# A feature network's large product recast as seven block products (one level of Strassen's algorithm)

## The reference

```python
w = jnp.einsum('bpf,mf->bpm', features, W_ft) + b_ft      # features (1024, 2, 5128), W_ft (512, 5128)
accumulator = stm * w                                     # stm (1024, 2, 1)
l1_x = jnp.clip(accumulator, 0.0, 1.0).reshape(features.shape[0], -1)
l2_x = jnp.clip(l1_x @ W1.T + b1, 0.0, 1.0)               # W1 (32, 1024)
return l2_x @ W2.T + b2                                   # W2 (1, 32)
```

## Time and profile before

| | |
|---|---|
| Time, median of 3 runs | 455.06 us (453.8 to 456.36) |
| Profiled execution, first to last instruction (span) | 452.5 us |
| Median of the runs less that span | 2.56 us |
| PE busy | 447.9 us (99%) |
| VectorE (DVE) busy | 178.2 us (39%) |
| ScalarE (ACT) busy | 132.3 us (29%) |
| Moved by DMA | 64.55 MB, mean 143 GB/s |
| Granted TensorE clock, mean | 0.999 |

### The profile page before, as it was taken

One profiled execution on the slowest core, in us unless ns is written; L12 is line 12 of the kernel. 1 busy time (PEld: TensorE's weight loads), 2 busy tenths in 40 slices (PEclk: granted clock), 3 DMA queues, 4 the chain that ended last, 5 costly groups with the idle time before them and its releaser, 6 DMA issues.

```text
span 452.5 us, 5442 instructions
## 1 busy us (share of the span) xinstructions
PE 447.9 (99%) x1996; PEld 365.8 (81%) x1996; DVE 178.2 (39%) x202; ACT 132.3 (29%) x167; POOL 14.6 (3%) x33
## 2 busy tenths in 40 slices
PE   8999999999999999999999999999999999999997
PEld 5888888888888888888888888888888888888883
DVE  3543333333333333563853333333333333333154
ACT  5443322222222233532133222222222333322101
POOL 4800000000000000000000000000000000000000
PEclk9999999999999999999999999999999999999999
DMA  7996454444454544444264444444444444440000
GB/s 288 240 370 210 139 139 139 145 143 152 142 152 144 150 152 139 139 141 139 70 211 140 141 140 143 150 146 148 144 151 152 148 139 139 139 139 0 0 1 0
DMA packets 24180, 64.55 MB, mean 143 GB/s; under 512 B 3172, under 2 KB 3436, under 8 KB 24044
## 3 DMA queue, kind: packets, MB, share of 16 engines
q1 hardware_dynamic: 23340, 62.93, 44.4%
q0 software_dynamic: 832, 1.51, 1.2%
HBM read 64.42 MB, written 0.00 MB: 142 GB/s over the span
## 4 chain that ended last, share of the span: by engine, by line
PE 98%; DMA 1%; ACT 0%; SPq 0%; DVE 0%; issue 0%
PE sums L309 96%; PE sums L343 1%; PE sums L395 1%; DMA x_raw<-x_t 1%; ACT part L234 0%; ACT x_hi L214 0%; PE sums L403 0%; SPq L149 0%; SPq L147 0%; PE sums L409 0%; DVE res L303 0%; DVE hid L299 0%
## 5 line engine op out<-in xcount | busy, mean ns | idle before, releaser
L309 PE MATMUL sums<-x_hi,w_hi 128*128 128x512 f32 x640 | 200.1, 389 | 0.5 <-ACT x_hi L214 0.5
L309 PE MATMUL sums<-x_hi,w_lo 128*128 128x512 f32 x640 | 199.7, 389 | 0.0
L309 PE MATMUL sums<-x_lo,w_hi 128*128 128x512 f32 x640 | 199.7, 389 | 0.0
L279 DVE TENSOR_TENSOR w_lo<-w_raw,w_hi 128x512 fp32r<-128x512 f32 x79 | 54.7, 693 | 222.3 <-ACT w_hi L222 222.3
L309 PEld LDWEIGHTS sums<-x_hi,w_hi 128*128 128x128 f32 x640 | 120.1, 188 | 26.7 <-ACT x_hi L214 0.8
L309 PEld LDWEIGHTS sums<-x_lo,w_hi 128*128 128x128 f32 x640 | 120.0, 188 | 25.1 <-issue 0.4
L309 PEld LDWEIGHTS sums<-x_hi,w_lo 128*128 128x128 f32 x640 | 120.1, 188 | 24.9
L222 ACT ACTIVATE w_hi<-w_raw 128x512 fp32r<-128x512 f32 x79 | 49.9, 631 | 280.5 <-PE sums L309 275.3
L282 DVE TENSOR_TENSOR x_lo<-x_raw,x_hi 128x1024 fp32r<-128x1024 f32 x79 | 96.8, 1226 | 26.7 <-ACT x_hi L224 26.3
L224 ACT ACTIVATE x_hi<-x_raw 128x1024 fp32r<-128x1024 f32 x79 | 82.6, 1046 | 8.6 <-DMA x_raw<-x_t 8.5
L250 DVE SCALAR_TENSOR_TENSOR act<-sums,b_ft_col,stm_all 128x512 f32<-128x512 f32 x16 | 12.0, 750 | 13.9 <-PE sums L309 13.7
(11 more groups left out here) (35 smaller groups left out, 23.2 us busy)
## 6 DMA issues: line engine op xcount, KB each, us to landing
x_raw<-x_t SPq DMA_DIRECT2D x79, 512.0 KB, 3.5
w_raw<-w_t SPq DMA_DIRECT2D x79, 256.0 KB, 2.7
stm_all<-stm POOLq DMA_DIRECT2D x1, 1024.0 KB, 12.0
x_raw<-x_t SPq DMA_DIRECT2D x2, 256.0 KB, 3.0
xr_raw<-x_t POOLq DMA_DIRECT2D x4, 64.0 KB, 7.5
w_raw<-w_t SPq DMA_DIRECT2D x1, 192.0 KB, 3.3
w_sb<-w_t POOLq DMA_DIRECT2D x1, 128.0 KB, 12.2
w_raw<-w_t SPq DMA_DIRECT2D x1, 64.0 KB, 1.9
```

Of the source, the lines that this page charges most:

```text
L279: nc.vector.tensor_tensor(w_lo[:, j, :], w_raw[:, j, :], w_hi[:, j, :].bitcast(F32), ALU.subtract).then_inc(w_lo_ready, 1)
L309: return nc.tensor.matmul(sums[:, m, c, :], w[:, j, m * P:(m + 1) * P], x[:, j, c * BANK:(c + 1) * BANK], **flags)
```

## The change

Of the 5128 features, 5120 are paired as 20 pairs of tiles of 128, and the 8 left over go in 16 matmuls as before (`K_PAIRS` = 20, `x_rest`). The 512 units are cut in two blocks of 256, the rows in two blocks of 1024. With A the weights (2x2 blocks, units by features) and B the features (2x2 blocks, features by rows), the product is made of seven block products instead of eight, in the form with shared block sums (Winograd's):

- Pass 0 (steps 0 to 19): A11 B11 in banks 0 to 3, and S1 T1 in banks 4 to 7, with S1 = A21 + A22, T1 = B12 - B11. VectorE also keeps S2 = S1 - A11 for all 20 pairs, and T1 stays in SBUF.
- Pass 1 (20 to 39): S2 T2 is added to banks 0 to 3, S3 T3 goes to banks 4 to 7, with S3 = A11 - A21, T3 = B22 - B12 and T2 = B22 - T1; T2 and T3 are made by one instruction of 2 x 1024 columns with B22 broadcast, and T2 takes T1's place.
- Pass 2 (40 to 59): (A12 - S2) B22 in banks 0 to 3 and A22 (B21 - T2) in banks 4 to 7.
- Pass 3 (60 to 69): the seventh product, A12 B21; a step takes two feature tiles of it.

A step is again 24 matmuls of 128x512, and there are 70 instead of 80. Each of the first 60 steps now has 512 columns of `w` and 2048 columns of `x` to round and to subtract (hi and lo), where a step of before had 512 and 1024. The raw ring has 4 slots (`RAW`), the hi ring 3 (`HI`), and the lo parts are written over the raw slots; so a load waits for TensorE to finish the step 4 earlier (`step_done`), no longer for VectorE. Loads of passes 0 to 2 are 1.44, 1.31 and 1.31 MB a step, of pass 3 1.31 MB. In DRAM the blocks lie beside each other for each feature row (`x_p`: rows of 16 KB, of which a DMA takes 4 or 8 KB; `w_p`: rows of 4 KB).

ScalarE drains the banks after each of passes 0 to 2, 8 copies from PSUM each; VectorE adds the blocks together in pass 2 and early in pass 3 (`combine`, `finish`). The first 3 steps are split in six half steps (`open_products`, order `OPEN_HALVES`, both sums of a step behind its plain half). Three quarters of the first small layer (12 of the 16 matmuls) come before the last step, the rest behind it. `stm` (1 MB, broadcast) is loaded by SP at step 50; GpSimd's 19 other DMAs wait until two steps are done.

The core of the diff:

```diff
+K_PAIRS = 20
+COLS = 1024
+MH = 256
+PASSES = 3
+STEPS = PASSES * K_PAIRS + K_PAIRS // 2
+OPEN = 3
+RAW = 4
+HI = 3
+OPEN_HALVES = ((0, 0), (1, 0), (0, 1), (2, 0), (1, 1), (2, 1))
+
+HALVES = (((0, 0, 0), (1, 1, 4)), ((1, 1, 0), (0, 0, 4)), ((1, 0, 0), (0, 1, 4)), ((0, 0, 0), (1, 1, 0)))
+
+
...
+            for g in range(OPEN, STEPS):
+                f, k = pass_of(g)
+                if g >= RAW:
+                    sp.wait_ge(step_done, g - RAW + 1)
+                i, j, n = raw_w(g, 0), raw_x(g, 0), g % RAW
+                if f == 0:
+                    sp.dma_start(ws[:, i:i + 3, :], w_p[k, :, 0:3, :]).then_inc(w_loaded[n], 16)
+                    sp.dma_start(xs[:, j, :], x_p[k, :, 0, :]).then_inc(x_loaded[n], 16)
+                    sp.dma_start(xs[:, TST + k, :], x_p[k, :, 1, :]).then_inc(t_loaded[n], 16)
+                elif f == 1:
+                    sp.dma_start(ws[:, i:i + 2, :], w_p[k, :, 0:2, :]).then_inc(w_loaded[n], 16)
+                    sp.dma_start(xs[:, j:j + 2, :], x_p[k, :, 1:3, :]).then_inc(x_loaded[n], 16)
+                elif f == 2:
+                    sp.dma_start(ws[:, i:i + 2, :], w_p[k, :, 2:4, :]).then_inc(w_loaded[n], 16)
+                    sp.dma_start(xs[:, j:j + 2, :], x_p[k, :, 2:4, :]).then_inc(x_loaded[n], 16)
...
+                if g == 2 * K_PAIRS + 10:
+                    sp.wait_ge(x_sum, 2 * K_PAIRS + 6)
+                    sp.dma_start(stm_all[:, :, :].rearrange("p h n -> p (h n)"),
+                                 stm.rearrange("(a n) -> a n", a=1).broadcast_to([P, 2 * COLS]))\
+                        .then_inc(stm_loaded, 16)
...
+            def sums_of(g):
+                f, k = pass_of(g)
+                i, j, n = raw_w(g, 0), raw_x(g, 0), g % RAW
+                opening = g < OPEN
+                dve.wait_ge(w_loaded[n], w_count(g))
+                if f == 0:
...
+                    nc.vector.tensor_tensor(ws[:, i + 1, :], ws[:, i + 1, :], ws[:, i + 2, :], ALU.add)\
+                        .then_inc(w_sum, 1)
...
+                    nc.vector.tensor_tensor(xs[:, TST + k, :], xs[:, TST + k, :], b11, ALU.subtract)\
+                        .then_inc(x_sum, 1)
...
+                    nc.vector.tensor_tensor(ws[:, KEPT + k, :], ws[:, i + 1, :], a11, ALU.subtract)\
+                        .then_inc(s_kept, 1)
+                elif f == 1:
+                    nc.vector.tensor_tensor(ws[:, i, :], ws[:, i, :], ws[:, i + 1, :], ALU.subtract)\
+                        .then_inc(w_sum, 1)
+                    dve.wait_ge(x_loaded[n], x_count(g))
+                    nc.vector.tensor_tensor(x_pair(g), xs[:, j + 1:j + 2, :].broadcast_to([P, 2, COLS]),
+                                            x_pair(g), ALU.subtract).then_inc(x_sum, 1)
+                elif f == 2:
+                    dve.wait_ge(s_kept, K_PAIRS)
+                    nc.vector.tensor_tensor(ws[:, i + 1, :], ws[:, i + 1, :], ws[:, KEPT + k, :], ALU.subtract)\
+                        .then_inc(w_sum, 1)
+                    dve.wait_ge(x_loaded[n], x_count(g))
+                    nc.vector.tensor_tensor(xs[:, j + 1, :], xs[:, j + 1, :], xs[:, TST + k, :], ALU.subtract)\
+                        .then_inc(x_sum, 1)
+
+            def low_step(g):
+                dve.wait_ge(s_kept, min(g + 1, K_PAIRS))
+                dve.wait_ge(w_hi_ready, later(g))
+                nc.vector.tensor_tensor(w_lo[:, g % RAW, 0:2, :], w_pair(g),
+                                        w_hi[:, g % HI, :, :].bitcast(F32), ALU.subtract).then_inc(w_lo_ready, 1)
+                dve.wait_ge(x_hi_ready, later(g))
+                nc.vector.tensor_tensor(x_lo[:, g % RAW, :, :], x_pair(g),
+                                        x_hi[:, g % HI, :, :].bitcast(F32), ALU.subtract).then_inc(x_lo_ready, 1)
...
+            sums_of(OPEN)
+            open_low(5, 2, 1)
+            third = 2 * K_PAIRS
+            fourth = 3 * K_PAIRS
+            for g in range(OPEN, STEPS):
+                if g + 1 < STEPS:
+                    sums_of(g + 1)
+                if g == 8:
+                    dve.wait_ge(rest_loaded, 16 * 8)
+                    nc.vector.tensor_tensor(wr_raw[:, 2, :], wr_raw[:, 2, :], wr_raw[:, 0, :], ALU.subtract)\
+                        .then_inc(rest_signed, 1)
+                low_step(g)
+                if g == 12:
...
+                    nc.vector.tensor_tensor(wr[64:P, :, :], wr_raw[64:P, :, :], wr[64:P, :, :].bitcast(F32),
+                                            ALU.subtract).then_inc(rest_ready, 1)
+                if g == third + 5:
+                    combine(3, c_all[:, 2, :], 1, 16)
+                if g == third + 8:
+                    dve.wait_ge(c_sum, 1)
+                    combine(3, c_all[:, 1, :], 2, 16)
+                if g == third + 16:
+                    finish(3, 1, 2)
+                if g == fourth + 2:
+                    combine(1, xs[:, TST:TST + 2, :].rearrange("p m n -> p (m n)"), 5, 24)
+                if g == fourth + 3:
+                    finish(1, 1, 5)
+                if g == fourth + 4:
+                    combine(2, xs[:, TST + 2:TST + 4, :].rearrange("p m n -> p (m n)"), 8, 24)
+                if g == fourth + 5:
+                    finish(2, 0, 8)
...
+            for b in range(4):
+                cols = slice(b * BANK, (b + 1) * BANK)
+                dve.wait_ge(bank_full, 7 * PASSES + b + 1)
+                nc.vector.scalar_tensor_tensor(out=c_all[:, 0, cols], in0=sums[:, b, :],
+                                               scalar=b_ft_col[:, b // 2:b // 2 + 1], in1=c_all[:, 0, cols],
+                                               op0=ALU.add, op1=ALU.add).then_inc(last_sum, 1)
+                dve.wait_ge(last_sum, 2 * b + 1)
+                nc.vector.tensor_tensor(c_all[:, 0, cols], c_all[:, 0, cols],
+                                        stm_all[:, 0, (b % 2) * BANK:(b % 2 + 1) * BANK], ALU.mult)\
+                    .then_inc(last_sum, 1)
+                dve.wait_ge(last_sum, 2 * b + 2)
+                nc.vector.tensor_scalar(c_all[:, 0, cols], c_all[:, 0, cols], 0.0, 1.0, ALU.max, ALU.min)\
+                    .then_inc(act_ready, 1)
+                if b == 1:
+                    hidden(0, 1)
...
+            def step(g):
+                f, k = pass_of(g)
+                h, r = g % HI, g % RAW
+                last = g == STEPS - 1 or (f < PASSES and k == K_PAIRS - 1)
+                for n, (wpos, xpos, bank) in enumerate(HALVES[f]):
+                    first = k == 0 and (n == 0 or f < PASSES)
+                    start = first and (f == 0 or f == PASSES or (f == 1 and bank == 4))
+                    if n == 0:
+                        pe.wait_ge(w_hi_ready, later(g))
+                        pe.wait_ge(x_hi_ready, later(g))
+                        if last:
+                            pe.wait_ge(w_lo_ready, later(g))
+                            pe.wait_ge(x_lo_ready, later(g))
+                    for m in range(2):
+                        for c in range(PERSP):
...
+                                pe.wait_ge(drained, 8 * (f - 1) + b + 1)
+                            product(b, w_hi, h, wpos, x_hi, h, xpos, m, c, start)
+                            if last and f < PASSES:
...
+                                mm = product(b, w_lo, r, wpos, x_hi, h, xpos, m, c, False, stop=True)
+                                if not (n == 1 and m == 1 and c == PERSP - 1):
+                                    mm.then_inc(bank_full, 1)
+                        if last and f < PASSES:
+                            continue
+                        if n == 0 and m == 0 and not last:
+                            pe.wait_ge(w_lo_ready, later(g))
+                            pe.wait_ge(x_lo_ready, later(g))
+                        for c in range(PERSP):
+                            product(bank + m * 2 + c, w_hi, h, wpos, x_lo, r, xpos, m, c, False)
+                        for c in range(PERSP):
+                            mm = product(bank + m * 2 + c, w_lo, r, wpos, x_hi, h, xpos, m, c, False)
+                mm.then_inc(step_done, 1)
+
...
+                for m in range(2):
+                    for c in range(PERSP):
+                        b = m * 2 + c
+                        for pos in range(2):
+                            product(b, w_hi, h, pos, x_hi, h, pos, m, c, False)
+                            product(b, w_hi, h, pos, x_lo, r, pos, m, c, False)
+                            product(b, w_lo, r, pos, x_hi, h, pos, m, c, False)
+                        nc.tensor.matmul(sums[:, b, :], wr[:, 3, m * P:(m + 1) * P],
+                                         xr[:, c * BANK:(c + 1) * BANK], start=False, stop=True,
+                                         skip_group_check=True).then_inc(bank_full, 1)
+                        if b == 0:
+                            add_halves(0, 1)
+                        if b == 2:
+                            second_layer(0, 1)
+
```

More of the change, by code:

```diff
@@ L27 @@
 P = 128
+BANK = 512
 WARM_UP = 8
```

(66 more changed lines are left out.)

517 lines of the change are left out of this document (300 added, 217 removed).

## The result

The changed kernel takes 431.8 us (430.98 to 432.28, 4 runs) against 454.91 for the kernel before; the ratio is 0.949 [0.947, 0.952]. The profiled execution has a span of 430.2 us. The forecast was 415, its range 408 to 427: right in direction, but 17 us too low, and outside the range.

A forecast was written before the change was run, and what follows sets the result against it. TensorE was taken as the bound nearly from end to end; 452.5 - 54.4 + 1.0 + 1.4 + 0.65 + 0.75 + 6.7 + 0.5 + 3.1 = 412.2 us of span, plus 2.6 for the median: 415 us, range 408 to 427.

The forecast's parts named there:

- Part 1: TensorE: 240 large matmuls fewer (70 steps for 80) at 0.2266 us each, -54.4 us.
- Part 2: VectorE's work per step against TensorE's 5.44 us: pass 1 tightest at 5.34; +1.0 us taken for pass 1.
- The first rival: VectorE bounds pass 1 at 5.86 us a step, total 422 us; chance 0.20.
- part 3: Loop of load, sums, lo parts, TensorE: must fit 11.33 us; pass 1 landing 5.3, total 10.4, slack 0.9.
- The second rival: Loads land later at 309 GB/s, total 424 us; sign: VectorE's sums wait for DMA every step; chance 0.12.
- Opening: Head and first steps, paced by landings and VectorE; step 3 ends at 34.6 us: +6.7 us.
- the upper bound: Opening's bound of 10 us, if a pause lets the clock fall to the 1.2 GHz level for some steps' parts.
- GpSimd's DMAs: 19 DMAs from 21.3 us slow loads 5 and 6: +0.5 us taken; at a quarter rate 2.4 us late.
- Left-over work: Left-over features at step 12: 3.4 us of VectorE work, less idle 0.8 and slack 1.2: +1.4 us.
- `combine` and `finish`: VectorE block additions in pass 2: `combine` at steps 45 and 48 costs 0, `finish` at 56 +0.65 us.
- `stm`: Its load on SP's queue at step 50 makes loads 2.6 us late, less 1.8 of slack: +0.75 us.
- Tail: Last step by bank, VectorE needing 2.0 us a bank, then the small layers: 10.8 us for 7.7, +3.1 us.

The follow-up runs named there:

- experiment 2: Changed kernel without loading B12 in pass 1 (0.79 MB a step, not 1.31; result not the product): 425.3 us, one run.
- experiment 1: Changed kernel with matmuls reordered within a step (8 hi by hi, 8 with w_lo, then 8 with x_lo): 415.5 us, ratio to before 0.9145.
- experiment 3: Changed kernel with VectorE making only T2 in pass 1 (1024 columns, T3 left out; loads stay): 430.2 us, one run.
- experiment 8: Changed kernel with x laid out in DRAM as block tiles of 512 KB in one piece: 426.0 us, ratio 0.938.
- experiment 5: Changed kernel with GpSimd's 19 DMAs waiting for 6 steps done, not 2, and left-over work 5 steps later: 433.9 us, one run.
- experiment 4: Changed kernel with the three left-over subtractions put behind steps 12, 14 and 16, not all behind 12: 428.1 us, ratio 0.942.
- experiment 6: Changed kernel with 18 idle matmuls ahead in place of 8: 429.7 us, one run.
- experiment 7: Changed kernel with x_lo matmuls last, also in passes' last steps, 18 idle matmuls, reordered opening, later GpSimd DMAs, left-over work in three parts: 415.7 us, ratio 0.915.
- experiment 10: Changed kernel with all combined: matmul order, x layout, 18 idle matmuls, reordered opening, earlier drains, GpSimd's DMAs and left-over work spread: 409.0 us, ratio 0.8995.

## Why the prediction was wrong

**Part 1 held.** 560 matmuls of each kind, steps of 5.44 us wherever nothing is late: -54.4 us.

**Part 2 held.** VectorE in pass 1 (start us, us), for the earlier trace rows:

```profile
161.28 0.42 DVE L381 TENSOR_TENSOR ws<-ws 128x256 f32<-128x256 f32 x1
161.62 2.28 DVE L384 TENSOR_TENSOR xs<-xs 128x2048 f32<-128x2048 f32 x1
163.82 0.68 DVE L397 TENSOR_TENSOR w_lo<-ws,w_hi 128x512 fp32r<-128x512 f32 x1
164.42 2.28 DVE L400 TENSOR_TENSOR x_lo<-xs,x_hi 128x2048 fp32r<-128x2048 f32 x1
166.62 0.42 DVE L381 TENSOR_TENSOR ws<-ws 128x256 f32<-128x256 f32 x1
```

0.34, 2.20, 0.60, 2.20: 5.34 us, to the hundredth. The fixed cost per instruction of the Trainium skill (VectorE: DVE Perf Modes, "The TRN2 errata") fits single durations (2.28), but here neighbours overlap by 0.08, so its 5.70 us a step did not come. The first rival, VectorE as the bound, was wrong in its mechanism too (experiment 2). That pass 1 has only 0.10 us of room for anything late was said, and not priced.

**The step that failed is part 3, the landing of the loads.** It was put at 5.3 us after the first issue of a step in pass 1. The row of the changed kernel (passes 1 and 2) says otherwise:

```profile
xs<-x_p SPq DMA_DIRECT2D x40, 1024.0 KB, 5.6
```

With the 0.4 us between the two issues that is 6.0 at the median, and single ones took up to 8 (in pass 1: 5.3/5.6/7.7 us, min/median/max, from the issue of x). So the slack of pass 1 was 0.2 us, not 0.9, and a late load went through to TensorE. Two errors lie in it. The rate of 397 GB/s was that of queues kept full; here most loads start in an empty queue, and the DMA engines are busy for 64% of the time from 126 to 232 us, most of pass 1. And I treated the landing as a constant. A loop with 1 us of slack turns the spread of landings into losses on one side only: early ones gain nothing, late ones cost. In pass 1 VectorE can make up only 0.10 us a step. So pass 1 cost 7.0 us for the 1.0 forecast, with no other work put into it. Experiments 1 and 2 show it from two sides, more slack for `x_lo` and smaller loads; experiments 3 (more idle time) and 8 (sooner landings) agree, with losses at the edge of what other kernels lost. Why single loads land late stays open; most of those that cost something had an instruction fetch beside them. The second rival (loads later, 424) was the nearest in mechanism, but by a lower rate for every load, and was given 0.12; its sign, a wait of VectorE's sums in every step of pass 1, came in 11 of 20. Taken one term after another:

- **Opening** (+8.9 for 6.7): TensorE ended step 0 at 16.65 for 15.9 and waited 3.0 us for step 3's `x_lo` (forecast 3.4), as foreseen. What I left to the upper bound is the clock, 1.7 us.
- **GpSimd's DMAs** (+3.0 for 0.5, with the first left-over work): load 6 took 11.9 us to land. The prediction's quarter rate (2.4 us) was nearer than the 0.5 taken. Experiment 5 shows that the loss goes with these DMAs.
- **Left-over work** (step 13: 4.4 for 1.4): the block met a slack already used up, and the clock added 1.7.
- **`combine` and `finish`** (1.0 and 2.3 for 0 and 0.65): the same slack. `stm` cost 0.4 for 0.75.
- **Tail** (+4.2 for 3.1): the schedule was right (VectorE 2.0 us a bank, the wait for the clip), small hops were missing.

**The clock was missing from the sum** as anything but a bound: 5.1 us. No row of before showed a fall, and TensorE hardly waited there; the change itself made the waits. The prediction allowed for a fall in the opening alone.

The Trainium skill (DMA: Bandwidth & Descriptors, "Latency and other measured facts") tells of rates halved by large power-of-two pitches. At 16 KB no run shows a halving; experiment 8 shows 0.4 us in 5.6 over all loads of x.

## What to carry to other kernels

When a change uses up the room of engines that had much of it, work out the slack of the loop that feeds the bound engine, and price it with the spread of the landings, not with a median or a bulk rate. If the spread is not at hand, look at which single loads are late and what runs beside them. Then look at what the bound engine asks for first: here putting the operand that is made last at the end of each step, at no cost, was worth 16 us, more than two thirds as much as the whole change (23 us). Stalls that have one cause don't add up, so fixes to it don't either.

## What the runs showed of the hardware

- Ahead of the tail, TensorE's granted clock fell to the 1.2 GHz level 15 times in the changed kernel and experiments 1 to 6 and 8, each time beside a wait of TensorE of 1.8 to 3.05 us; each of the three in the changed kernel cost about 1.7 us. So a stall can cost almost twice its length. But the length of the wait alone does not tell: waits of 2.06 us (changed kernel, at 345 us), 2.04 (experiment 7), 2.4 (experiment 2, at 92 us) and 2.7 us (experiment 6, at 92 us) had no fall beside them.
- In the ten kernels of this case in which GpSimd issues its 19 small DMAs (0.66 MB) in one bunch, steps 4 to 12, beside it, lost 1.0 to 7.3 us (3.0 in the changed kernel, 1.0 in experiment 8), some of it by the clock and the first left-over work; with the DMAs spread over 15 steps, in experiment 10, they lost nothing.
- Loads of x in pass 1 landed 5.3 to 7.7 us after their issue in the same loop. Those with an instruction fetch of 8 or 16 KB in their first 3.5 us landed later (in four kernels 6.5 us at the median, last packet, for 5.6), and the steps behind them had 18.1 of 23.7 us of the losses. That the fetch is the cause was not tested.
